# A four-layer graph network: the message multiply moves to GpSimd, and 96 more pointer columns per partition are placed by TensorE

## What is computed

```python
# layer 0 (2 heads x 32)            en = feat_src[src]; ev = feat_dst[dst]
e     = sum(leaky_relu(en + ev) * attn, -1)          # one score per edge and head
alpha = softmax of e over the edges of one dst
msg   = softmax(en * r_feat * alpha, axis=-1)        # softmax over 32 features
rst   = (feat + segment_sum(msg, dst).sum(heads)) @ W1 + b1
# layer 1                           segment_sum(h[src], dst)
# layer 2                           per-edge MLP weights, tensor product, segment_sum over dst
# layer 3 (4 heads)                 softmax over the edges of one src, of a_src[src] + a_dst[dst]
```

## Time and profile before

| | us |
|---|---|
| median of 3 runs | 10080.78 (10080.61 to 10084.44) |
| the profiled execution, whole | 10082.84 |
| its span, first to last instruction | 10081.0 |
| mean granted TensorE clock | 0.683 |
| busy: TensorE 4719.6, VectorE 7132.4, ScalarE 3441.0, GpSimd 7227.2 | |

### The profile page before, as it was taken

One profiled execution on the slowest core, in us unless ns is written; L12 is line 12 of the kernel. 1 busy time (PEld: TensorE's weight loads), 2 busy tenths in 40 slices (PEclk: granted clock), 3 DMA queues, 4 the chain that ended last, 5 costly groups with the idle time before them and its releaser, 6 DMA issues. The chain is left out here.

```text
span 10081.0 us, 82596 instructions
## 1 busy us (share of the span) xinstructions
PE 4719.6 (47%) x24537; PEld 2705.5 (27%) x24537; DVE 7132.4 (71%) x11645; ACT 3441.0 (34%) x4798; POOL 7227.2 (72%) x7493
## 2 busy tenths in 40 slices
PE   3348000004642477777548888888533676200002
PEld 2347000001111366666413333333211333100002
DVE  8984999668966544444349999999633777588862
ACT  0016444223421366666412222222100121277750
POOL 5777777775446777777777777777677777777767
PEclk6559555555655688888768888888666888655555
DMA  7212666533324111111111111111110111144432
GB/s 262 84 39 70 248 250 248 184 117 111 132 74 139 28 27 27 29 27 27 28 37 31 29 29 30 29 29 31 25 18 18 56 45 40 57 141 140 142 109 53
DMA packets 469603, 815.78 MB, mean 81 GB/s; under 512 B 232261, under 2 KB 329974, under 8 KB 418598
## 3 DMA queue, kind: packets, MB, share of 16 engines
q10 hardware_dynamic: 81600, 447.60, 11.5%
q0 software_dynamic: 239424, 156.62, 7.8%
q1 hardware_dynamic: 148134, 206.27, 6.1%
HBM read 402.58 MB, written 407.28 MB: 80 GB/s over the span
## 5 line engine op out<-in xcount | busy, mean ns | idle before, releaser
L1576 POOL DMA_INDIRECT hs<-tab_h,src_i x3136 | 3008.1, 959 | 988.7 <-issue 947.2
L1191 POOL DMA_INDIRECT en<-tab_s,src_i x1568 | 1487.5, 949 | 557.6 <-issue 476.7
L1855 PE MATMUL tp_ps<-w_pair,x 128*128 128x512 f32 x1568 | 999.2, 724 | 15.2 <-DVE prod_b L1983 15.2
L2260 POOL DMA_INDIRECT rows_src<-out_rows,pos x784 | 764.3, 975 | 254.2 <-issue 241.0
L2272 POOL DMA_INDIRECT hs<-tab_h,ptr x784 | 742.8, 947 | 238.9 <-issue 238.9
L1076 DVE SCALAR_TENSOR_TENSOR picked<-rank_ps,hot_hi 128x98 f32<-128x98 f32 x1568 | 312.2, 255 | 735.3 <-PE rank_ps L981 718.2
L2282 PE MATMUL late_ps<-hot_col,hot_row 128*128 128x512 f32 x928 | 574.5, 705 | 532.2 <-DVE hot_col L2361 514.4
L977 PE MATMUL rank_ps<-place_sb,hot_t 128*128 128x98 f32 x3136 | 663.9, 323 | 0.0
L815 PE MATMUL turn<-ident,tot 128*2 128x128 f32 x2 | 0.7, 373 | 1260.5 <-DVEq L841 1260.5
L1107 POOL DMA_INDIRECT by_src<-ends_ahead,pos_ahead x320 | 339.0, 1060 | 306.3 <-PE fresh L1451 181.9
L783 DVE TENSOR_TENSOR_SCAN sheld<-skeep,sheld 128x1088 f32<-128x1088 f32 (+1 forms) x196 | 377.4, 1926 | 233.1 <-ACT sheld L775 232.8
(11 more groups left out here) (394 smaller groups left out, 14838.7 us busy)
## 6 DMA issues: line engine op xcount, KB each, us to landing
sums<-rows ACTq DMA_DIRECT2D x98, 1088.0 KB, 4.2
sums<-rows ACTq DMA_DIRECT2D x147, 512.0 KB
ev_rows<-zeros ACTq DMA_DIRECT2D x16, 3136.0 KB
en_rows<-en SPq DMA_DIRECT2D x49, 1024.0 KB
raw<-ev_rows ACTq DMA_DIRECT2D x49, 1024.0 KB, 4.8
en_back<-en_rows ACTq DMA_DIRECT2D x49, 1024.0 KB
r<-in_edge_attr_2x ACTq DMA_DIRECT2D x49, 1024.0 KB
y_rows<-r ACTq DMA_DIRECT2D x49, 1024.0 KB
```

The lines of the kernel that those rows point to most:

```text
L1191: pool.indirect_dma_start(en[s][:, g, :], None, tab_s0, bass.IndirectOffsetOnAxis(ap=src_i[:, p * 2 * CH + g:p * 2 * CH + g + 1], axis=0)) ...
L1576: pool.indirect_dma_start(rows[k][:, g, :], None, tab_h, bass.IndirectOffsetOnAxis(ap=src_i[:, t * CH + g:t * CH + g + 1], axis=0)).then_i ...
L1855: nc.tensor.matmul(o, x2[k][:, a, b * EP:(b + 1) * EP], w3_cols, start=True, stop=False)
L2260: pool.indirect_dma_start(rows_src, bass.IndirectOffsetOnAxis(ap=pos2[s][:, g:g + 1], axis=0), out_rows[s][:, g, :], None).then_inc(sent_r ...
```

## The change

The multiply by `alpha` leaves VectorE and becomes one GpSimd instruction a chunk, reading `alpha` where it lies in SBUF; `z` has four buffers for three. Of the ranked pointers, fourteen chunks for twenty are ranked in layer 0, four for five are scattered in the scoring block, and the other ten (160 columns) are spread between the multiplies, one or two scatters after each. The six chunks more that are left (`LATE = 560` columns for 464) are ranked in layer 1, which counts four for three a chunk, and placed by TensorE in layer 3, 150 of them ahead of the first pair for 60. `pos_col` is written over `pos_late`.

```diff
-        AHEAD, SENT = 20, 5
+        AHEAD, SENT = 14, 4
...
-            z = [sb(st, f"z{n}", [EP, CH, 64]) for n in range(3)]
+            ZS = 4
+            z = [sb(st, f"z{n}", [EP, CH, 64]) for n in range(ZS)]
...
             @block.gpsimd
             def _(pool):
-                for t in range(SENT, AHEAD):
-
-                    K.wait(pool, "pool", added, 6 * (t - SENT) - 5)
-                    send_ahead(pool, t)
+                to_send = (AHEAD - SENT) * CH
+                sent_by = lambda t: SENT * CH + t * to_send // (2 * PAIRS)
+
+                def weigh(t, p, s, k):
+
+                    if k == 0:
+                        K.wait(pool, "pool", rows_in[s], p * 8 + (16 - 8 * s))
+                    K.wait(pool, "pool", added, t - ZS + 1)
+                    at = alpha[:, :, cols(t)].rearrange("p h c -> p c h").unsqueeze(3).to_broadcast([EP, CH, HEADS0, FEAT])
+                    nc.gpsimd.tensor_tensor(heads(z[t % ZS][:, :, :]), heads(y_in[s][:, k * CH:(k + 1) * CH, :]), at, ALU.mult).then_inc(weighted, 1)
+
+                def body(p, s):
+                    for k in range(2):
+                        t = 2 * p + k
+                        weigh(t, p, s, k)
+                        send_columns(pool, sent_by(t), sent_by(t + 1))
+                turns(body)
                 pool.wait_ge(sent_ahead, 16 * CH * AHEAD)
...
                 def stage(p, s, k):
                     t = 2 * p + k
-                    if k == 0:
-
-                        K.wait(dve, "dve", rows_in[s], p * 8 + (16 - 8 * s))
-                    c.step(nc.vector.tensor_copy(weight[k], alpha[:, :, cols(t)].rearrange("p h c -> p c h")))
-                    nc.vector.tensor_tensor(heads(z[t % 3][:, :, :]), heads(y_in[s][:, k * CH:(k + 1) * CH, :]), per_head(weight[k]), ALU.mult).then_inc(weighted, 1)
                     if t:
                         divide(t - 1, 1 - k)
...
-            EACH = 3
+            EACH = 4
...
-                return min(LATE, 60 + 9 * p)
+                return min(LATE, 150 + 9 * p)
```

More of the change, by code:

```diff
@@ L1103, in build, with send_columns @@
         sent_ahead = K.own("sent_ahead")
-        def send_ahead(pool, t):
-            for n in range(t * CH, (t + 1) * CH):
+        def send_columns(pool, first, end):
+            for n in range(first, end):
                 pool.indirect_dma_start(by_src, bass.IndirectOffsetOnAxis(ap=pos_ahead[:, n:n + 1], axis=0),
@@ L1212, in _ @@
                 for t in range(SENT):
-                    send_ahead(pool, t)
+                    send_columns(pool, t * CH, t * CH + CH)
             @block.scalar
@@ L1419, in build, with heads @@
             per_edge = lambda at: small_ps[:, at:at + CH * HEADS0].rearrange("p (c h) -> p c h", h=HEADS0)
-            z_div, weight = per_edge(128), [per_edge(160 + 32 * k) for k in range(2)]
+            z_div = per_edge(128)
             S = RowSums(st, sums)
+            def heads(ap):
+                return ap.rearrange("p c (h f) -> p c h f", h=HEADS0)
             rows_in = [K.sem(f"rows_in{s}") for s in range(2)]
@@ L1450, in add_heads @@
                     for n in range(HEADS0):
-                        last = nc.tensor.matmul(S.message(k), ident[0:EP, 0:EP], z[t % 3][:, :, n * FEAT:(n + 1) * FEAT].rearrange("p c f -> p f c"),
+                        last = nc.tensor.matmul(S.message(k), ident[0:EP, 0:EP], z[t % ZS][:, :, n * FEAT:(n + 1) * FEAT].rearrange("p c f -> p f c"),
                                                 start=n == 0, stop=n == HEADS0 - 1)
@@ L1462, in exps @@
                     K.wait(act, "act", weighted, t + 1)
-                    nc.scalar.activation(z[t % 3][:, :, :], z[t % 3][:, :, :], ACT.Exp).then_inc(exped, 1)
+                    nc.scalar.activation(z[t % ZS][:, :, :], z[t % ZS][:, :, :], ACT.Exp).then_inc(exped, 1)
                 for t in range(2 * PAIRS):
@@ L1486, in per_head @@
                     return ap.unsqueeze(3).to_broadcast([EP, CH, HEADS0, FEAT])
-                def heads(ap):
-                    return ap.rearrange("p c (h f) -> p c h f", h=HEADS0)
                 def divide(t, k):
-                    z_t = z[t % 3]
+                    z_t = z[t % ZS]
                     K.wait(dve, "dve", exped, t + 1)
@@ L2195, in build @@
                 pos_row = sb(time, "pos_row", [EP, LATE])
-                pos_col = sb(time, "pos_col", [EP, LATE])
                 late_dst = sb(time, "late_dst", [EP, LATE])
@@ L2351, in _ @@
                 c.step(nc.vector.tensor_scalar(pos_row[:, :], pos_row[:, :], -NEAREST, None, ALU.add))
-                c.step(nc.vector.scalar_tensor_tensor(pos_col[:, :], pos_row[:, :], -float(HCOLS), pos_late[:, :], ALU.mult, ALU.add))
+                c.step(nc.vector.scalar_tensor_tensor(pos_late[:, :], pos_row[:, :], -float(HCOLS), pos_late[:, :], ALU.mult, ALU.add))
                 c.restart()
@@ L2360, in late @@
                         nc.vector.tensor_scalar(hot_row[n % 2][:, :], count_up[:, 0:EP], pos_row[:, n:n + 1], late_dst[:, n:n + 1], ALU.is_equal, ALU.mult)
-                        nc.vector.tensor_scalar(hot_col[n % 2][:, :], count_up, pos_col[:, n:n + 1], None, ALU.is_equal).then_inc(late_hot, 1)
+                        nc.vector.tensor_scalar(hot_col[n % 2][:, :], count_up, pos_late[:, n:n + 1], None, ALU.is_equal).then_inc(late_hot, 1)
                 late(0, late_by(0))
```

## The result

The changed kernel takes 10002.8 us (median of 4 runs, 9998.5 to 10005.1) where the kernel before took 10080.7 on the same chip (4 runs): a ratio of 0.9922, 95% interval 0.9906 to 0.9937, 78 us faster. The forecast was 9996, its range 9958 to 10036. The profiled execution has a span of 9999.8 us for 10081.0.

The account below looks back on a forecast made before the run. VectorE was taken to bound the message block, GpSimd most other blocks. Terms -75.5 - 20.4 + 3.9 + 6.7 = -85.3 us took 10082.8 to 9997.5, given as a 9996 us median; range 9958 to 10036.

Parts of the forecast that it names:

- Message block: VectorE loses copy and multiply, the fresh buffer's loop then sets 5.20 us a chunk: -75.5 us (bounds -57 and -136).
- so I expect some high stretches to reach the matmuls, and take 5.20 us: Message block: TensorE's shorter pauses let some 2.4 GHz clock reach the head sums; period 5.20 us for 5.986.
- 5.29 and 5.39: Message block: the fresh buffer's loop period from trace rows, 5.39 us where the four matmuls end 0.1 us later.
- Rival B: Message block: TensorE gets 2.4 GHz for most matmuls; period 4.6 to 4.9 us, total 9938 to 9967; chance 0.10.
- VectorE's 4.58 us: Message block: VectorE's remaining work a chunk, the period's bound if the matmuls got short.
- The multiply: Message block, GpSimd: taken as 2.4 us (1.5 to 4.7), cost 0; the bound at 3.1, no gain at 3.9.
- rival D: Message block: the multiply is so long that GpSimd sets a period over 6.29 us, total near 10148 at worst; chance 0.07.
- Rival E: Message block: GpSimd's multiply locks out VectorE's two-SBUF-input `so_far`; period 6.7 us, mild case 5.9 to 6.25; chance 0.05.
- Scoring block: GpSimd's tail ends 22.7 us earlier, less 2.3 us for a stretched scatter: -20.4 us (bounds 16 and 23).
- Layer 1: Extra ranking hides behind the gathers; only GpSimd's early wait for a fourth count costs 3.9 us (bounds 0 and 8).
- Layer 3: 90 more columns precede pair 0, ready 13 us early; the pairs' lost lead costs 6.7 us (bounds 0 and 20).
- the clock term: Message block: the high TensorE clock was expected to shorten the head sums, giving a period of 5.20 us.

Follow-up runs that it names:

- fill_pe: The changed kernel with six small bf16 matmuls into a spare PSUM bank behind each head sum: 9999.6 us, no change.
- straight_heads: The changed kernel with the head sums' moving operand read in its own order, without the stride (sums of other columns): 10025.7 us (0.9941).
- two_multiplies: The changed kernel with a second GpSimd multiply a chunk into a spare buffer that nobody reads: 10058.3 us (0.9979).
- pointers_alone: The kernel before with only the pointers' new split, the multiply staying on VectorE: 10070.1 us (0.9985).
- multiply_alone: The changed kernel with the pointers split as before, so only the multiply moves to GpSimd: 10024.5 us for 10086.2 (0.9939).
- before_both: The kernel before with a second fresh buffer and a second buffer for the stored rows: 10077.6 us for 10079.8 (0.9997).
- two_fresh_stores: The changed kernel with two fresh buffers and two buffers for stored rows: 13080.5 us beside a kernel before of 13071.8; message block 519.7 us.

## Why the prediction was right

The mechanism held, and the range with it. That the total came within 7 us is in part luck: the largest term was 16.5 us too large, and two smaller terms and a difference in a block that was not touched gave 12 back.

- **Message block, -75.5 us predicted, -59.0 measured.** The mechanism held: VectorE's list handed the limit to the fresh buffer's loop. The size was off at one step, "so I expect some high stretches to reach the matmuls, and take 5.20 us". TensorE's waits for the scan did fall as foreseen (160.0 / 97 = 1.65 us a chunk), but the high level gives these matmuls only 0.1 us per head sum (`fill_pe`). The rows' own 5.29 and 5.39 were the answer: the mean is 5.368. 97 x 0.168 = 16.3 us of the 16.5 missed.
- **Rival B** could not come about in this kernel: at 2.4 GHz the strided matmul is as slow as at 1.2 (0.861 us, `fill_pe`), and only without the stride is it faster (`straight_heads`). I had read the low clock as the reason for 0.86 us. The trace of the kernel before could have told: in four of its head sums the second matmul ran at the high level throughout, and the third still started 0.860 to 0.862 us after it.
- **VectorE's 4.58 us** was right as a bound: with the loop opened and `so_far` out of the way the period is 4.53 us.
- **The multiply** took 1.96 us; I had taken 2.4 from bounds of 1.5 and 4.7, and the estimate from the Trainium skill ("GPSIMD Engine Reference", section "Elementwise — side-by-side cycle accounting") was 2.25. All three lie under the 3.1 us at which it matters, and `two_multiplies` confirms GpSimd's sum: with w = 3.96 the block is as long as before, which was put at 3.9. No run passes it, so rival D's slower kernel itself was not seen.
- **Rival E** was priced by its right mechanism, and set aside for the right reason in this kernel (two chunks of 98). With 240 scatters for 160 it already strikes seven times. It came with the next step: two fresh buffers moved `so_far` into the multiply, and of the 0.84 us a chunk between 5.37 and 4.53 the buffers gave 0.18, and the other 0.66 came when it was moved.
- **Scoring block, -20.4 predicted, -24.1 measured** (first `y` load 2293.30 for 2317.40; -24.9 with the pointers alone). No scatter was left to be stretched beside VectorE's last instruction at 2285.14; the 2.3 us that I held back came too, and 1.4 more, which is outside the bounds of 16 and 23: the block closes 4.7 us behind VectorE's last instruction, and 11.4 us behind GpSimd's last scatter for 12.8 before.
- **Layer 1, +3.9 predicted:** its gathers last 4.3 us longer, 3.8 with the pointers alone; one wait, as foreseen.
- **Layer 3, +6.7 predicted:** +3.7 us measured, +4.6 with the pointers alone. Pair 0's lead was 12.9 us for 13, and the lost lead of the pairs comes out in one wait of 9.99 us at pair 10, where the kernel before has none. Of the 3.0 us missed the shorter scatters, which the sum did not have, can explain the 0.9 between the two kernels; the rest stays open. The sum itself was loose: 7579.74 + 138.6 is 7718.3 and not 7718.7, and 7760.4 - 7753 is 7.4, from which 6.7 does not follow.
- Between the profiled executions 81.2 us are gone for 85.3 predicted: 16.5 less than forecast came from the message block, 3.7 and 3.0 more from the scoring block and layer 3, and 5.2 us from layer 2, whose gathers took 2005.1 us before and 1999.8 after; 0.4 went to layer 1, and 0.9 is spread over the rest. The piece of layer 2 is no effect of the change: these gathers take 2002.5 in `pointers_alone`, 2003.8 in `multiply_alone`, and 1999.6 in `before_both`, which has neither half.
- **Signs that missed.** The period of 5.37 is just over the 5.1 to 5.35 forecast, the block of 537 us just over 520 to 535, VectorE's wait before the add 0.85 us for 0.4 to 0.7, the multiply under its 2.2 to 2.6, and layer 3 under its 5 to 9. All but the last two are the clock term again.

## What to carry to other kernels

When a bound is taken off one engine, look for two consecutive iterations in the old trace in which that work is already missing: their period is the new one, and no hoped-for clock should be added to it without a row of the same instruction, shape and stride at the other level. An instruction moved to GpSimd can stall a small VectorE instruction with two SBUF inputs, as it did `so_far`. Whether it does depends on phases, so ask again after each further change of pace, and put the small instruction where no multiply runs, or only its end. The longest wait in the list (here 203 us for a store) need not be a bound; only opening each loop tells.

## What the runs showed of the hardware

- A GpSimd multiply of 128x1024 fp32, one operand broadcast over 32 features, takes 1.96 us beside scatters, matmuls and VectorE's work (1956 to 1997 ns in the 98 instructions of the changed kernel).
- Fp32 matmul records of 512 columns whose moving operand has a stride of 64 floats follow each other at 0.861 us at either level of the clock (`fill_pe`); with runs of 32 neighbouring floats at 0.853 us at 1.2 GHz and 0.429 at 2.4 GHz (`straight_heads`).
- A VectorE instruction of 0.20 us with two SBUF inputs that a GpSimd multiply holds ends 0.04 to 0.06 us after the multiply's end. It can be recorded before the multiply, by 0.12 us in the changed kernel and by 0.66 in `multiply_alone`, where it lasts 2.68 us, the longest of all runs. A multiply of VectorE with one input in PSUM keeps its 1.22 us beside GpSimd's (`two_fresh_stores`).
- An indirect scatter issued right behind a multiply comes 0.16 us after it and lasts 1.00 us; behind another scatter 0.30 and 0.96. The 11 ns by which scatters differ between kernels stay open.
